# A language-model tower: the place of ScalarE's copies of the turned normed rows in slots 7 and 0 of a group

## The chip, the cores and the metric

The kernel runs on one core of one Trainium2 chip. The metric is the device time in microseconds (us), median of 3 runs. TensorE is called PE, VectorE DVE, ScalarE ACT, GpSimd POOL and SyncE SP.

## The reference

32 sequences of 128 tokens with 192 features go through an embedding with layer norm and four residual layers, each on the layer norm of the rows. Everything is fp32. The change lies in the stage that computes the first two and the first half of the third:

```python
h = tok_ref(x, mask, tok_w, pos_w, type_w, gamma, beta)              # embedding, layer norm
h = h + attn_ref(layernorm(h), Wq, Wk, Wv)                           # one head, causal
h = h + soft_experts(layernorm(h), phi, ln_g, ln_b, w1, b1, w2, b2)  # 64 experts x 16 slots
h = h + attn12(layernorm(h), w_qkv, w_proj, b_proj)                  # 12 heads, rotary
h = h + routed_experts(layernorm(h), router_w, w1, b1, w2, b2)       # 8 experts, top 1

# soft_experts, first half
phi_n  = phi * rsqrt(sum(phi**2, axis=0) + 1e-6)
logits = einsum('bmd,npd->bmnp', x, phi_n)       # 1024 slots (columns) per token
D      = softmax(logits, axis=1)                 # over the tokens
C      = softmax(logits, over all 1024 slots)    # used at the end of the layer
Xs     = einsum('bmd,bmnp->bnpd', x, D)          # the slots' inputs, then 64 experts, then C
```

## The kernel before, in words

The program has four stages one after the other: the tower (`tower_phase`, to about 338 us), the 64 soft experts, the combine and twelve-head attention stage, and the 8 routed experts. Only the tower is touched.

The 32 sequences are 8 groups of 4. The 1024 slots of the soft experts are 8 columns of 128. `each_slot` walks `t` from 0 to 11 and within each `t` eight places `s` from 0 to 7, which are called slots of the group here. At one `t` three groups are in work: `e = t` is embedded and normed, `a = t - 1` goes through the attention, `x = t - 2` gets the layer norm for the soft experts. Beside them one column runs per slot, in three steps: `n0` (its logits are made), `n1 = n0 - 1` (its weights are transposed), `n2 = n0 - 2` (the slots are summed). The first column begins at t = 2, s = 5. Every engine has its own program with the same walk and a function `slot`, and its instructions run in the order written there; engines meet only at semaphores.

What PE does in a slot, in this order: `logits_of(n0)` (five matmuls of 512 columns into bank 0 or 6, line 115 through the helper `matmuls`), `turn_weights(n1)` (four transposes into bank 1, L1050; waits for ACT's exponentials of the slot before), `slot_sums(n2)` (L1057; waits for ACT's copy of the transposed weights and for `stage_ready`, ACT's copy of the sums of the slot before), and after that what the attention needs: in slot 1 `queries`, in slot 2 `scores`, and so on. At the end of slot 6 it calls `turn_x(e, 0)`, and at the end of slot 7 `turn_x(e, 1)`: four transposes each (L955) of the normed rows `xn` (named e_rows in the trace) into bank 5, first the first 128 features, then the last 128 (64 and a repeat of them). Both use the same bank, so `turn_x(e, 1)` waits until ACT has copied the first half out (`pe.wait_ge(xT_took, 2 * e + 1)`). From t = 4 on, slot 0 ends with `turn_max` (L1027, `f = t - 4`), which also writes bank 5 and waits until ACT has copied the second half (`pe.wait_ge(xT_took, 2 * min(f + 4, NG))`).

What ACT does in a slot, in this order: `evict`, then for the column `take_turned(n1)` (copy of the transposed weights, L895), `exps(n0)` (four exponentials, L879; waits for DVE's column maximum `col_max`), `keep_logits(n0)` (L889), `take_sums(n2)` (L901, named slot_stage). In slot 7 `evict` holds the copy of the first half of the turned rows (L842, named e_x_full<-bank, semaphore `xT_took`); in slot 0 of the next `t` it holds the copy of the second half (L842) and then the rounding of both halves into `xThi` (L851, named e_x_hi, 1,024 columns, semaphore `xT_hi_ready`). In slots 2 to 6 it holds other copies.

What DVE does in slot 0, in this order: the column maximum (L760), the running maximum (L737), then `attn(a, 0)` (L681 and L682; waits for `xT_hi_ready`, makes `xT_split` for PE's `queries` in slot 1), then the statistics of group x and of group e (L619 to L624), which POOL turns into reciprocal roots. Slot 1 begins again with a column maximum (L760), on which ACT's exponentials of slot 1 wait. SP stores the kept logits and the slot sums as ACT makes them.

There are no columns in t = 0 and t = 1 at s = 7, and none in t = 1 and t = 2 at s = 0.

Of the kernel before, what the change touches and what calls it, by code (L numbers as in the profile page):

```python
# [97 lines left out]
def round_rest(act, stacked, rest):  # L98

    two = rest.rearrange("p (i n) -> p i n", i=2)  # L100
    act.activation(even(stacked[0:DR]), two[0:DR], ACT.Copy)
    return act.activation(odd(stacked[DR:P]), two[DR:P], ACT.Copy)
# [311 lines left out]
def tower_phase(nc, ins, T, small):  # L414
# [4 lines left out]
    with ExitStack() as ctx:  # L419
# [96 lines left out]
        with nc.Block() as block:  # L516
# [304 lines left out]
            def _(act):  # L821
# [18 lines left out]
                def take(ready, value, out, src, took):  # L840
                    act.wait_ge(ready, value)
                    act.activation(out, src, ACT.Copy).then_inc(took, 1)  # L842

                def evict(e_before, e, a, x, s):
                    if s == 7 and e is not None:
                        past(act, v_done, 2 * e)
                        take(xT_done, 2 * e + 1, xT[:, 0, :], b5, xT_took)
                    if s == 0 and e_before is not None:
                        take(xT_done, 2 * e_before + 2, xT[:, 1, :], b5, xT_took)
                        act.wait_ge(xT_took, 2 * e_before + 2)  # L850
                        act.activation(xThi[:], xT[:], ACT.Copy).then_inc(xT_hi_ready, 1)  # L851
                    if s == 2 and a is not None:
                        past(act, score_done, a)
                        take(q_done, 2 * a + 1, qT0[:], b7, q_took)
                    if s == 2 and a is not None:
                        take(q_done, 2 * a + 2, qT1[:], b4, q_took)
                    if s == 3 and x is not None:

                        past(act, logits, NC * (x - 1))
                        take(x3T_done, 2 * x + 1, T["x_hi"][x % 2][:], b5, x_hi_took)  # L860
                    if s == 4 and x is not None:
                        past(act, logits, NC * (x - 1))
                        act.wait_ge(x3T_done, 2 * x + 2)
                        round_rest(act, T["x_hi_over_lo"][x % 2], b5[:, 0:2 * P]).then_inc(x_hi_took, 1)
                    if s == 4 and a is not None:
                        past(act, av_done, 2 * a)
                        take(v_done, 2 * a + 1, v[:, 0:2, :], pair(b4), v_took)
                    if s == 5 and a is not None:
                        take(v_done, 2 * a + 2, v[:, 2:4, :], pair(b7), v_took)
                    if s == 6 and a is not None:  # L870
                        take(pT_done, a + 1, pT[:], b7, pT_took)

                def exps(n):
                    act.wait_ge(col_max, n + 1)

                    past(act, turned, n - 1)
                    for j in range(GB):
                        js = slice(j * P, (j + 1) * P)
                        last = act.activation(ls[:, n % 2, js], logits_bank(n)[:, js], ACT.Exp,  # L879
                                              bias=nmc[:, n % 2, j:j + 1])  # L880
                    last.then_inc(exped, 1)

                def keep_logits(n):
                    if n == 2:
                        act.wait_ge(T["xm_filled"], 16 * NE1 * CAP // (4 * P))
                    past(act, kept_stored[n // 2 % 3], 16 * (n // 6))

                    past(act, run_max_ready, run_maxes(n - 5) if n > 5 else 0)
                    act.activation(kept_columns(n), group4(logits_bank(n)), ACT.Copy).then_inc(kept_ready, 1)  # L889

                def take_turned(n):
                    act.wait_ge(turned, n + 1)

                    past(act, sums_done, n - 1)
                    act.activation(disp[:, n % 2, :], b1, ACT.Copy).then_inc(disp_ready, 1)  # L895

                def take_sums(n):
                    act.wait_ge(sums_done, n + 1)

                    past(act, stored[n % 3], 16 * (n // 3))  # L900
                    act.activation(stage[:, n % 3, :, :].rearrange("p (k j) d -> p k j d", k=2), U,  # L901
                                   ACT.Copy).then_inc(stage_ready, 1)

                def slot(t, s, e, a, x, n0, n1, n2, f):
                    evict(a, e, a, x, s)
                    if n1 is not None:
                        take_turned(n1)
                    if n0 is not None:
                        exps(n0)
                        keep_logits(n0)  # L910
                    if n2 is not None:
                        take_sums(n2)
                    if s == 3 and a is not None:
                        act.wait_ge(score_max, a + 1)
                        past(act, pT_done, a)
                        for j in range(GB):
                            last = act.activation(ex[:, j, :], sm[:, j, :], ACT.Exp, bias=nmx[:, j:j + 1],
                                                  accum_out=ssum[:, j:j + 1])
                        last.then_inc(exp_done, 1)
                    if t == LAST and s == 6:  # L920
                        small.first_take(act, 0, (b4, b7))
                        small.first_w1_hi(act)
                    if t == LAST and s == 7:
                        small.first_take(act, 1, (b4, b7))
                    if (s, e) in ((7, 1), (1, 2)):
                        k = e - 1
                        act.wait_ge(phi_scaled, k + 1)
                        act.activation(T[f"phi_hi{k}"][:], T[f"phiT{k}"][:], ACT.Copy).then_inc(phi_hi_ready, 1)

                each_slot(slot)  # L930
                act.wait_ge(nm_turned, 1)
                act.activation(nm_rows[:], b5[0:NB, 0:P], ACT.Copy).then_inc(nm_rows_ready, 1)
# [170 lines left out]
def past(eng, sem, value, wait=None):  # L1103

    if not isinstance(value, int) or value > 0:
        if wait:
            wait(eng, sem, value)
        else:
            eng.wait_ge(sem, value)
# [964 lines left out]
```

## Time and profile before

| | us |
|---|---|
| median of 3 runs | 1396.27 (1396.11 to 1398.48) |
| the profiled execution, device time | 1397.63 |
| its span in the trace | 1395.9 |
| busy in the span: PE / PEld / DVE / ACT / POOL | 1320.4 / 1175.0 / 974.7 / 951.6 / 253.5 |
| mean granted PE clock | 0.981 of full |

PEld is PE's weight load, which runs beside its matmuls. A row of the timeline gives the start of an instruction or of a run of equal ones, its length, engine, source line, output and inputs; in brackets stands how long the engine was idle before it and what released it. The end of a matmul is modelled, and matmuls overlap, so the distance of two starts says more than the lengths. A helper's line (L115, L842) stands for several callers; the tile's name tells them apart. Some tiles of the tower use buffers of the later stage and carry their names (e_x_full, e_x_hi, e_rows).

### The profile page before, as it was taken

The page shows a single profiled execution, that of the slowest core. Times are in us where ns is not written, and L with a number is a line of the kernel's source. Part 1 is how long each engine was busy: PE and PEld are TensorE (multiplying, and loading weights), DVE is VectorE, ACT ScalarE, POOL GpSimd, SP SyncE. Part 2 cuts the span into 40 slices and gives each one's busy share as a digit, 9 for nine tenths or more (in the row PEclk, how much of TensorE's full clock was granted, in tenths as well). Part 3 has the DMA queues.
Part 4 walks back from the last instruction along what each step waited for, and adds up shares of the span by engine and source line. Part 5 has one row for each costly group of instructions (what it writes and reads, how often), then busy time and mean ns, then how long its engine had stood idle before and what let it go on. Part 6 is the DMA issues. An engine that isn't in the chain of part 4 may idle for free. (4 is left out here: it accounts for less than half of the span.)

```text
span 1395.9 us, 29574 instructions
## 1 busy us (share of the span) xinstructions
PE 1320.4 (95%) x8926; PEld 1175.0 (84%) x8926; DVE 974.7 (70%) x2977; ACT 951.6 (68%) x2361; POOL 253.5 (18%) x284
## 2 busy tenths in 40 slices
PE   8799999998999999999999999799999999879995
PEld 6578888886898998998998998689889889768895
DVE  7888888555777777777777773688888888632331
ACT  1488888887676666666666663588888888735551
POOL 5321200000111111111111110012212212211344
PEclk9899999999999999999999999999999999989998
DMA  6144444455666666666666665545545547015641
GB/s 202 41 151 164 163 152 152 158 194 187 187 199 199 192 196 196 193 197 198 192 196 196 195 185 180 153 137 159 161 137 156 157 132 216 16 47 126 151 72 17
DMA packets 179715, 219.99 MB, mean 158 GB/s; under 512 B 23428, under 2 KB 146538, under 8 KB 179616
## 3 DMA queue, kind: packets, MB, share of 16 engines
q1 hardware_dynamic: 146224, 178.61, 41.6%
q10 hardware_dynamic: 25712, 33.19, 7.1%
q0 software_dynamic: 7680, 6.95, 2.5%
q8 instruction: 52, 0.85, 0.3%
q14 instruction: 47, 0.39, 0.1%
HBM read 141.31 MB, written 79.90 MB: 158 GB/s over the span
## 5 line engine op out<-in xcount | busy, mean ns | idle before, releaser
L1296 PE MATMUL bank<-e_w,e_h_full 128*128 128x192 f32 x1920 | 324.7, 326 | 0.4
L1296 PEld LDWEIGHTS bank<-e_w,e_h_full 128*128 128x128 f32 x1920 | 310.6, 190 | 1.7 <-ACT e_h_full L1370 1.3
L1370 ACT ACTIVATE e_h_full<-bank,e_b 128x512 f32<-128x512 f32 x240 | 165.2, 689 | 166.0 <-PE bank L115 166.0
L1234 POOL TENSOR_TENSOR e_ln_rstd<-e_ln_var_eps,minus_half 128x4 f32<-128x4 f32 x62 | 62.5, 1008 | 440.8 <-DVE e_ln_var_eps L1420 440.8
L1777 ACT ACTIVATE probs<-bank,head_neg_max 128x128 f32<-128x128 f32 x384 | 134.9, 392 | 7.8 <-DVE head_neg_max L1873 5.8
L1427 DVE TENSOR_SCALAR e_rows<-e_slot_sums,e_ln_mean_var,e_ln_rstd 128x192 f32<-128x192 f32 x248 | 77.5, 376 | 77.6 <-POOL e_ln_rstd L1234 77.6
L1339 ACT ACTIVATE e_x_full<-bank,e_ln_shift,e_ln_gain 128x512 f32<-128x512 f32 x124 | 76.5, 667 | 42.9 <-issue 37.6
L1057 PE MATMUL bank<-x,dispatch_weights 128*128 128x193 f32 x512 | 96.0, 329 | 7.2 <-ACT slot_stage L901 6.2
L115 PE MATMUL bank<-e_x_hi,e_w1hi 128*128 128x512 f32 x216 | 98.0, 454 | 2.7 <-ACT e_h_full L1370 1.7
L1657 PE MATMUL bank<-slot_outputs_then_w_part,combineT 128*128 128x193 f32 x512 | 92.5, 333 | 2.5 <-ACT combineT L1769 2.1
L1057 PEld LDWEIGHTS bank<-x,dispatch_weights 128*128 128x128 f32 x512 | 82.3, 190 | 11.2 <-issue 11.2
L1657 PEld LDWEIGHTS bank<-slot_outputs_then_w_part,combineT 128*128 128x128 f32 x512 | 83.1, 189 | 9.0 <-issue 9.0
L760 DVE TENSOR_REDUCE column_neg_max<-bank 128x4 f32<-128x512 f32 x64 | 44.2, 691 | 65.9 <-PE bank L115 65.4
L1777 ACT ACTIVATION_READ_ACCUMULATOR probs<-bank,head_neg_max 128x1 f32 x384 | 89.1, 232 | 0.0
L879 ACT ACTIVATE slot_exp<-bank,column_neg_max 128x128 f32<-128x128 f32 x256 | 72.9, 374 | 22.1 <-DVE column_neg_max L760 22.0
L1454 DVE TENSOR_TENSOR e_stage<-bank,e_b 128x768 f32<-128x768 f32 x64 | 61.3, 958 | 35.4 <-PE bank L1296 35.3
L115 PE MATMUL bank<-e_x_hi_over_lo,e_w1hi 128*128 128x512 f32 x216 | 86.0, 398 | 0.0
L115 PE MATMUL bank<-e_x_hi,e_w1lo 128*128 128x512 f32 x216 | 85.5, 396 | 0.0
L115 PE MATMUL bank<-e_x_lo,e_w1hi 128*128 128x512 f32 x216 | 85.4, 396 | 0.0
L115 PE MATMUL bank<-e_x_hi_over_lo,e_w1lo 128*128 128x512 f32 x216 | 85.1, 394 | 0.0
L1602 POOL TENSOR_TENSOR ln_rstd<-ln_var_eps,minus_half 128x1 f32<-128x1 f32 x64 | 35.9, 561 | 211.0 <-DVE ln_var_eps L1942 153.8
L122 PE MATMUL bank<-spare_operand 128*128 128x512 f32 x229 | 64.1, 428 | 8.4 <-PEq L1558 4.2
(286 smaller groups left out, 3127.7 us busy)
## 6 DMA issues: line engine op xcount, KB each, us to landing
slot_sums<-slot_stage SPq DMA_DIRECT2D x64, 386.0 KB, 3.2
e_slot_sums<-slot_sums SPq DMA_DIRECT2D x64, 386.0 KB, 3.6
slot_outputs<-e_stage ACTq DMA_DIRECT2D x64, 384.0 KB, 3.6
slot_outputs_then_w_part<-slot_outputs SPq DMA_DIRECT2D x32, 768.0 KB
e_w<-in_w SPq DMA_DIRECT2D x64, 288.0 KB, 2.9
slot_logits<-kept_logits SPq DMA_DIRECT2D x32, 512.0 KB
slot_logits<-slot_logits SPq DMA_DIRECT2D x32, 512.0 KB, 3.4
e_w1raw<-in_w SPq DMA_DIRECT2D x80, 192.0 KB, 2.7
```

Of the source, the lines that this page charges most:

```text
L115: last = pe.matmul(out, w, m, start=n == 0, stop=n == len(pairs) - 1, **kw)
L122: pe.matmul(out, T["spare"][:, 0:P], T["spare"][:], start=True, stop=True)
L879: last = act.activation(ls[:, n % 2, js], logits_bank(n)[:, js], ACT.Exp, bias=nmc[:, n % 2, j:j + 1])
L1057: last = pe.matmul(U[:, j // 2, j % 2, :], disp[:, n % 2, j * P:(j + 1) * P], x3[n // NC % 3][:, j, 0:1 + D], start=True, stop=True)
L1234: pool.tensor_tensor(rs[u][:], ve[u][:], half[:], ALU.pow).then_inc(rstd_ready, 1)
L1296: last = pe.matmul(ybank(u)[:, j // 2, (j % 2) * D:(j % 2 + 1) * D], hf[:, k, js], w2s[u][:, k, :], start=k == 0, stop=k == MT - 1)
L1339: last = act.activation(xf[:, k, 0:c], bank[:, k, 0:c], ACT.Identity, bias=lnb[:, k, ds(n, 1)], scale=lng[:, k, ds(n, 1)])
L1370: act.activation(hf[:, m, :], hbank(u, m), act_fn, bias=b1s[:, m, ds(n, 1)]).then_inc(acted, 1)
L1427: last = dve.tensor_scalar(rows[u][:, j, :], features_of(sums[u], j), mv[u][:, j, 0:1], rs[u][:, j:j + 1], ALU.subtract, ALU.mult)
L1454: dve.tensor_tensor(y_out[:, part], y_in[:, part], b2s[u][:].unsqueeze(1).unsqueeze(1) .broadcast_to([P, 2 // halves, 2, D]), ALU.add).the ...
L1657: last = pe.matmul(bank[:, 0, 0:D + 1], cT[:, c, :], ysb[u][:, c, :], start=c == 0, stop=c == NC - 1)
L1777: last = act.activation(pr[:, s, g, :], bank[:, 4 + s, g * P:(g + 1) * P], ACT.Exp, bias=nmx[:, s, g:g + 1], accum_out=esum[:, s, g:g + 1])
```

## The change

ACT's `slot` calls `evict` at the head of a slot. Now it does so in slots 1 to 6 only; in slots 7 and 0 it calls it behind the four column steps. No instruction, buffer, semaphore or wait value is added or removed, and the other engines' programs are the same.

```diff
                 def slot(t, s, e, a, x, n0, n1, n2, f):
-                    evict(a, e, a, x, s)
+                    if s not in (0, 7):
+                        evict(a, e, a, x, s)
                     if n1 is not None:
                         take_turned(n1)
                     if n0 is not None:
                         exps(n0)
                         keep_logits(n0)
                     if n2 is not None:
                         take_sums(n2)
+                    if s in (0, 7):
+                        evict(a, e, a, x, s)
                     if s == 3 and a is not None:
```

## Rows read from the trace of the kernel before

**Rows 1.** One stretch: length; busy (instructions) of PE, PEld, DVE, ACT, POOL; PEclk; DMA; GB/s.

```profile
150.00:200.00 50.00, 47.30 (x299) 42.52 (x297) 42.43 (x123) 40.85 (x104) 9.03 (x9) 1.00 0.44 160
```

**Rows 2.** Waits, 0 to 480 us: total us, times, longest us.

```profile
PE bank L1057 <- ACT slot_stage L901: 6.2, 10, 1.0
...
PE bank L955 <- ACT e_x_full L842: 0.7, 1, 0.7
```

**Rows 3.** Timeline of ACT, t = 5 slot 7 to t = 6 slot 1.

```profile
177.63 0.60 ACT L842 ACTIVATE e_x_full<-bank 128x512 f32<-128x512 f32 x1 [0.29 <-PE bank L955]
179.17 0.60 ACT L895 ACTIVATE dispatch_weights<-bank 128x512 f32<-128x512 f32 x1 [0.94 <-PE bank L1050]
...
181.14 0.85 ACT L901 ACTIVATE slot_stage<-bank 128x772 f32<-128x772 f32 x1
181.84 0.65 ACT L842 ACTIVATE e_x_full<-bank 128x512 f32<-128x512 f32 x1
182.51 1.06 ACT L851 ACTIVATE e_x_hi<-e_x_full 128x1024 fp32r<-128x1024 f32 x1
183.48 0.58 ACT L895 ACTIVATE dispatch_weights<-bank 128x512 f32<-128x512 f32 x1
...
185.43 0.85 ACT L901 ACTIVATE slot_stage<-bank 128x772 f32<-128x772 f32 x1
...
189.07 1.15 ACT L879 ACTIVATE slot_exp<-bank,column_neg_max 128x128 f32<-128x128 f32 x4 [2.30 <-DVE column_neg_max L760]
```

**Rows 4.** Timeline of PE, the same slots to slot 2.

```profile
178.97 1.48 PE L1057 MATMUL bank<-x,dispatch_weights 128*128 128x193 f32 x8
180.28 0.60 PE L955 MATMUL bank<-ident,e_rows 128*128 128x128 f32 x4
...
181.88 0.60 PE L1050 MATMUL bank<-ident,slot_exp 128*128 128x128 f32 x4
...
183.63 0.60 PE L1027 MATMUL bank<-ident,running_max 128*128 128x128 f32 x4
...
186.43 1.55 PE L1057 MATMUL bank<-x,dispatch_weights 128*128 128x193 f32 x8 [0.60 <-ACT slot_stage L901]
187.68 0.53 PE L115 MATMUL bank<-e_x_hi,M_hi 128*128 128x512 f32 x1
...
191.55 1.55 PE L1057 MATMUL bank<-x,dispatch_weights 128*128 128x193 f32 x8
```

**Rows 5.** Timeline of DVE, slots 0 and 1.

```profile
183.61 0.69 DVE L681 TENSOR_TENSOR e_x_lo<-e_x_full,e_x_hi 128x512 fp32r<-128x512 f32 x1 [0.24 <-ACT e_x_hi L851]
...
188.34 0.69 DVE L760 TENSOR_REDUCE column_neg_max<-bank 128x4 f32<-128x512 f32 x1
```

**Rows 6.** Timeline of ACT, t = 3 slot 0 (first) and t = 8 slot 1.

```profile
76.67 1.06 ACT L851 ACTIVATE e_x_hi<-e_x_full 128x1024 fp32r<-128x1024 f32 x1
...
258.26 0.84 ACT L901 ACTIVATE slot_stage<-bank 128x772 f32<-128x772 f32 x1
```

**Rows 7.** Timeline of DVE, t = 3 slot 0.

```profile
79.12 0.69 DVE L681 TENSOR_TENSOR e_x_lo<-e_x_full,e_x_hi 128x512 fp32r<-128x512 f32 x1
```

**Rows 8.** Timeline of PE, t = 8 slot 2.

```profile
260.70 1.48 PE L1057 MATMUL bank<-x,dispatch_weights 128*128 128x193 f32 x8
```

**Rows 9.** Timeline of PE, three of its pauses, elsewhere in the span.

```profile
48.68 0.79 PE L115 MATMUL bank<-e_x_hi,M_hi 128*128 128x512 f32 x1 [2.40 <-DVE e_x_hi_over_lo L682]
...
885.86 0.88 PE L1702 MATMUL bank<-ident,qk_padded 128*128 128x128 f32 x6 [2.19 <-DVE qk_padded L1949]
...
1208.62 0.62 PE L115 MATMUL bank<-onehot,upto 128*128 128x128 f32 x2 [2.14 <-ACT probs L1777]
```

**Rows 10.** Stretches behind these pauses, columns as in rows 1.

```profile
51.00:52.00 1.00, 1.00 (x4) 0.82 (x3) 1.00 (x2) 0.29 (x1) 0.69 (x2) 0.64 0.09 28
886.00:888.00 2.00, 2.00 (x13) 1.74 (x13) 0.68 (x2) 0.81 (x1) 0.81 (x4) 1.00 0.34 109
1210.00:1212.00 2.00, 2.00 (x11) 2.00 (x10) 0.55 (x2) 1.18 (x2) 0.44 (x2) 0.50 0.00 0
```

## The prediction, on record before the changed kernel was run

> **What bounds the kernel now.** I read the page's first part, then the waits of the first third, then the timelines of ACT, PE and DVE over one turn of the tower, from slot 7 of one t to slot 2 of the next. The first part has PE busy for 95% of the span, and a stretch in the tower shows the same, 47.30 of 50 us at a granted clock of 1.00 [rows 1]; an edit on ACT costs or gains only through what PE then waits for. In the waits of the tower the largest one of PE on ACT is for the copy of the slot sums, 6.2 us in ten waits. For the copy that the change moves, PE waited once, 0.7 us [rows 2]. So the copies sit well today, and the wait that the change could shorten is worth 6.2 us at the very most.
>
> The timelines show the order in time. In slot 7 ACT copies the first half at 177.63, right after PE has turned it, and then sits idle for 0.94 us until PE has transposed the column's weights; the column work starts at 179.17 [rows 3]. PE comes to the second half's transposes at 180.28, long after the copy's end at 178.23, and goes through without a pause [rows 4]. In slot 0 the second copy starts at 181.84, the rounding ends at 182.51 + 1.06 = 183.57, and DVE takes it at 183.61: DVE was waiting for it, 0.24 us [rows 3, 5]. From there a chain runs on DVE to the column maximum of slot 1 at 188.34, for which ACT's exponentials wait 2.30 us [rows 3, 5]. The copy of the sums behind them lets PE's slot sums of slot 2 start at 191.55 [rows 4]. So two things end on the moved instructions: PE directly, through bank 5, and that chain through DVE.
>
> **The change, slot 7.** Nothing is added or removed. The first copy now stands behind the four column steps. Those can't start sooner: what they wait for is PE's transposes at 179.17, and ACT was idle ahead of them [rows 3]. So the gain on ACT is nothing, the 0.60 us of the copy merely leave an idle place. The copy starts where the last column step lets it, at 181.84 (the copy behind the same step in slot 0 started then [rows 3]), and ends at 182.44. From ACT's end to PE's start I take 0.15 us: the copy of the sums ends at 185.43 + 0.85 = 186.28 and PE starts at 186.43 [rows 3, 4]. PE's second transposes therefore start at about 182.60 in place of 180.28, 2.32 us later. PE has nothing else to do: its slot sums are over at 178.97 + 1.48 = 180.45 [rows 4], the transposes are next in its order, and all of the next slot's logits are queued behind them. That is a pause of 2.15 us.
>
> **The change, slot 0.** PE's transposes of the column's weights ended at 181.88 + 0.60 = 182.48, 2.20 us after the second half's began [rows 4]. Now they end at 182.60 + 2.20 = 184.80, and ACT's column work starts at 184.84. It was at 183.48, because the second copy and the rounding stood ahead of it; the move gains 1.0 us here against the transposes' end, and loses it again at once. The column work takes 181.84 - 179.17 = 2.67 us from its first start to the next instruction's [rows 3], so the second copy starts at 187.51. From its start to the end of the rounding it takes 183.57 - 181.84 = 1.73 us [rows 3], so the rounding ends at 189.24, 5.67 us later than before.
>
> PE is done with slot 0's sums by 180.45 + 3.35 + 2.32 = 186.12 (3.35 us is the distance from 180.28 to 183.63, one slot of PE [rows 4]) and `turn_max`, next in its order, waits for the second copy: 187.51 + 0.64 + 0.15 = 188.30 in place of 183.63. That is a second pause, of 2.18 us. The 0.60 us pause ahead of slot 1's sums goes [rows 4], since the copy of the sums now ends earlier, at 187.6. PE's queries in slot 1 come at 188.30 + (187.68 - 183.63) - 0.76 = 191.59, where 0.76 is that pause seen from the start that it would otherwise have had. They need DVE's two instructions, over 1.4 us behind the rounding at 190.7, and don't wait. PE alone would be 3.91 us late.
>
> But the DVE chain decides. It starts 5.67 us later, and it had no pause to give back but the one at its head: the maximum of slot 1 moves from 188.34 to 194.01, ACT's exponentials from 189.07 to 194.74, and PE's sums of slot 2 from 191.55 to 197.22, with two short pauses ahead of them. From slot 2 on all three engines are late by the same 5.67 us, and PE is back to running without slack; there is nothing left to catch up with. POOL's roots, the gathers and SP's stores hang on these engines and move along; no DMA is issued from ACT here.
>
> **How often.** A slot 7 and the next slot 0 with column work occur in six pairs: t = 2/3 to t = 7/8. In t = 0 and 1 there are no columns and the order is as it was. Four pairs are as worked out, 22.7 us. In the first pair DVE took the rounding only at 79.12 though it was ready at 76.67 + 1.06 = 77.73 [rows 6, 7]: 1.35 us of cover beyond the hand-over, so 4.32 us. In the last pair there is no group to embed any more, DVE's chain is shorter, and PE's sums of slot 2 at 260.70 did not wait: the copy ahead of them ended at 258.26 + 0.84 = 259.10 [rows 6, 8]. That is 1.45 us of cover after the hand-over: 4.22 us. Sum: 31.2 us.
>
> **The clock.** The tower runs at the full granted clock [rows 1], and the change puts twelve pauses of 2.15 to 2.18 us in. Three pauses of that size stand in the trace [rows 9]: after 2.40 us at 48.68 and after 2.14 us at 1208.62 PE came back at the lower level, 1.2 GHz (0.64 in the mean of 51 to 52, 0.50 at 1210 to 1212), after 2.19 us at 885.86 at the full one, 2.4 GHz [rows 10]. Two of three came back low, so I take the clock to fall in four of the six pauses in slot 7. The low stretch after 48.68 lasted to about 51.7 (a mean of 0.64 is 0.72 us at half), so 3.0 us in which 1.5 us of work is lost. There it all lies on the path, since ACT's column work waits for PE's transposes: 4 x 1.5 = 6.0 us. Bounds: 0 and 9.0. After the pause in slot 0 PE has 5.67 - 3.91 = 1.76 us of slack against the DVE chain, which covers the 1.5 us: nothing.
>
> By the Trainium skill (TensorE: Matmul & The Clock Gate, Why this matters for your kernels) only pauses longer than these need be avoided to hold the full clock; by that the sum would stay at 31.2. Two of the three rows above speak against it, one for it, so it is a rival below.
>
> **The sum.** 31.2 + 6.0 = 37.2 us. On the profiled execution, 1397.63, that gives 1434.8; it was 1.36 us above the median of its runs, so on the median 1396.27 it is 1433.5. I say 1433.
>
> **Rivals.**
> - The clock holds in all twelve pauses: 1396.3 + 31.2 = 1427.5. For it: the pause at 885.86 [rows 9]. Against: the two others.
> - The clock falls in all six slot-7 pauses, and sometimes in slot 0 beyond the slack: 31.2 + 9.0 + about 2 = 42, 1438.5.
> - Only PE's own waits count and DVE's chain catches up: six times 3.91, 23.5 us, 1419.8. Against: DVE waited at the head of its 4.73 us from 183.61 to 188.34, and ACT at their end [rows 3, 5].
> - Other sign, faster: in slot 0 ACT's column work no longer stands behind 1.73 us of copies. The copy of the sums would end 1.0 us earlier and the 0.60 us pause ahead of slot 1's sums would go, with no loss elsewhere: 6 x 0.6 = 3.6 us, 1392.7. It decides on one point: whether the first copy is done when PE comes to the second transposes, at 180.28. It would have to be 2.2 us earlier than the order on ACT lets it.
> - The change does nothing, because PE's pauses fall on time that it had idle anyway: 1396.3. The trace shows no such idle time at 180.28 or 183.63 [rows 4].
>
> **How the numbers follow.** Forecast (2 to 5 falls of the clock) 0.53, clock holds 0.22, clock falls always 0.15, PE alone 0.06, no change 0.02, faster 0.02. The forecast's case spans 1429 to 1437; the range takes in the neighbours less the ends, 1424 to 1440. A change of 0.2%, 2.8 us, is about what can be told from none. Slower by more than that has 0.96, within it 0.02, faster 0.02.
>
> **What would show it.** In the trace after: six waits of PE at L955 and five at L1027 (from t = 4 on) on ACT's e_x_full, each 2.0 to 2.3 us; the copy of slot 7 right behind slot_stage; ACT idle ahead of the weights' copy in slot 0; DVE idle some 3.6 us ahead of L681 (0.24 + 5.67 - 2.32); the distance of two e_x_hi starts 5.7 us longer than before, more where the granted clock shows 0.5; the stages after the tower as long as before. It is wrong if the L955 waits are missing or well below 2 us, if the period grows by some 4 us only (then DVE's chain had slack), or if the clock costs over 2 us a pair.

## The result, and the profile after

The changed kernel takes 1437.22 us (median of 4 runs, 1432.4 to 1438.73) against 1397.38 for the kernel before beside it: ratio 1.0284, 95% interval 1.0263 to 1.0304, some 39.8 us slower. The forecast was 1433, in a range of 1424 to 1440. The profiled execution took 1438.32 us, its span is 1436.6, 40.7 more than before. ACT's first gelu of the experts starts at 383.2 in place of 343.6, so 39.6 us of that were lost in the tower; the stages behind it lost 1.1 us, which I don't explain. That is less than the executions of one kernel differ by (1396.1 to 1401.7 for before).

The profile page's first part, columns as in the table of before. PE's idle time grew by 28.0 us (103.5 against 75.5). The other 12.7 us are PE being busy for longer with as many instructions, at a mean granted clock of 0.975 in place of 0.981; ACT and DVE did the same work as before.

```profile
PE 1333.1 (93%) x8926; PEld 1183.0 (82%) x8926; DVE 974.0 (68%) x2977; ACT 950.1 (66%) x2361; POOL 252.5 (18%) x284
```

The waits of the changed kernel from 0 to 500 us, columns as in [rows 2]. Before, the first was 1.8 us in six waits, the second 0.7 us in one (the same one stands here as the seventh, beside six of 2.08 us), the third did not occur, and the fourth was 0.7 us in one. Line numbers behind the change are three higher than before, so L958 are the transposes of the normed rows, L1030 is `turn_max`, L1053 the transposes of the weights and L1060 the slot sums. The last line shows what the change saved: the old wait for slot_stage fell from 6.2 to 4.6 us.

```profile
DVE e_x_lo L681 <- ACT e_x_hi L851: 23.3, 7, 4.0
...
PE bank L958 <- ACT e_x_full L842: 13.2, 7, 2.1
...
PE bank L1030 <- ACT e_x_full L842: 10.1, 5, 2.2
...
PE bank L1053 <- ACT slot_exp L879: 5.6, 4, 2.0
...
PE bank L1060 <- ACT slot_stage L901: 4.6, 8, 1.0
```

One pair of slots in the timeline of the changed kernel, t = 3 slot 7 to t = 4 slot 1, first PE. It answers to [rows 4].

```profile
112.87 1.48 PE L1060 MATMUL bank<-x,dispatch_weights 128*128 128x193 f32 x8
116.42 0.66 PE L958 MATMUL bank<-ident,e_rows 128*128 128x128 f32 x4 [2.08 <-ACT e_x_full L842]
...
122.16 0.63 PE L1030 MATMUL bank<-ident,running_max 128*128 128x128 f32 x4 [2.17 <-ACT e_x_full L842]
...
131.07 1.55 PE L1060 MATMUL bank<-x,dispatch_weights 128*128 128x193 f32 x8 [0.32 <-ACT slot_stage L901]
```

The same pair on ACT, answering to [rows 3]. The copy of slot 7 stands right behind slot_stage and PE's transposes start 0.05 us after its end; then ACT idles 2.34 us, because PE's next weights come late. In slot 0 the same happens again.

```profile
115.03 0.85 ACT L901 ACTIVATE slot_stage<-bank 128x772 f32<-128x772 f32 x1
115.73 0.64 ACT L842 ACTIVATE e_x_full<-bank 128x512 f32<-128x512 f32 x1
118.71 0.60 ACT L895 ACTIVATE dispatch_weights<-bank 128x512 f32<-128x512 f32 x1 [2.34 <-PE bank L1053]
...
121.37 0.64 ACT L842 ACTIVATE e_x_full<-bank 128x512 f32<-128x512 f32 x1
122.05 1.06 ACT L851 ACTIVATE e_x_hi<-e_x_full 128x1024 fp32r<-128x1024 f32 x1
...
128.60 1.14 ACT L879 ACTIVATE slot_exp<-bank,column_neg_max 128x128 f32<-128x128 f32 x4 [2.38 <-DVE column_neg_max L760]
```

And on DVE, answering to [rows 5]. It idles 3.57 us for the rounded rows (0.24 before), and its 4.73 us to the next column maximum are as long as they were.

```profile
118.28 0.69 DVE L760 TENSOR_REDUCE column_neg_max<-bank 128x4 f32<-128x512 f32 x1 [2.84 <-PE bank L115]
...
123.14 0.69 DVE L681 TENSOR_TENSOR e_x_lo<-e_x_full,e_x_hi 128x512 fp32r<-128x512 f32 x1 [3.57 <-ACT e_x_hi L851]
...
127.87 0.69 DVE L760 TENSOR_REDUCE column_neg_max<-bank 128x4 f32<-128x512 f32 x1
```

The granted clock (the third number from the right) in eight stretches of the changed kernel, columns as in [rows 1]. Four of the six pauses in slot 7 were followed by the lower level (158, 202, 244, 288); those that ended at 76.07 and 116.42 were not. The stretch at 124 follows the pause ahead of turn_max. Two more, at 174 and 260, follow pauses in slot 2, one pair of which stands in the PE lines below the table.

```profile
116.00:118.00 2.00, 1.57 (x9) 1.39 (x10) 0.00 (x0) 0.37 (x1) 0.00 (x0) 1.00 0.50 198
124.00:126.00 2.00, 2.00 (x8) 1.70 (x8) 1.90 (x9) 0.38 (x1) 0.00 (x0) 0.50 0.16 57
158.00:160.00 2.00, 2.00 (x7) 1.51 (x6) 0.07 (x1) 0.00 (x0) 0.00 (x0) 0.50 0.05 19
174.00:176.00 2.00, 2.00 (x9) 1.91 (x9) 2.00 (x5) 1.14 (x4) 0.00 (x0) 0.52 0.50 198
202.00:204.00 2.00, 2.00 (x8) 1.62 (x7) 0.53 (x1) 0.00 (x0) 0.00 (x0) 0.50 0.02 8
244.00:246.00 2.00, 2.00 (x8) 1.51 (x8) 0.35 (x1) 0.00 (x0) 0.00 (x0) 0.56 0.00 0
260.00:262.00 2.00, 2.00 (x11) 1.91 (x10) 2.00 (x6) 1.24 (x5) 0.00 (x0) 0.50 0.19 67
288.00:290.00 2.00, 2.00 (x9) 1.80 (x8) 1.29 (x2) 0.57 (x2) 0.00 (x0) 0.50 0.00 0
```

```profile
172.12 0.66 PE L1053 MATMUL bank<-ident,slot_exp 128*128 128x128 f32 x4 [1.44 <-ACT slot_exp L879]
173.41 2.26 PE L1060 MATMUL bank<-x,dispatch_weights 128*128 128x193 f32 x8 [0.62 <-ACT slot_stage L901]
```

The distance of two roundings (e_x_hi, L851 here) is the tower's period and the best ruler for what follows. This table is made from the timelines of ACT; the first column is the kernel before, the others are what each kernel of the next section adds to it. I call a period clean when no stretch of low clock lies in it that delays it.

```
rounding t ->  before  changed  slot 7  slot 0  filled  stats  filled+stats  behind exps
3 -> 4          36.04    +4.32   +0.88   +3.15   +5.94  +1.23         +1.29        +0.02
4 -> 5          34.73    +7.25   +3.42   +5.00   +5.65  +6.69         +3.48        +0.79
5 -> 6          35.07    +8.56   +2.92   +3.35   +7.25  +4.07         +3.51        +0.78
6 -> 7          34.72    +7.18   +1.94   +3.33   +5.60  +3.44         +3.47        +0.77
7 -> 8          34.72    +8.49   +1.99   +5.02   +5.66  +6.29         +3.50        +0.82
```

### The profile page after: what moved, and what is told of

Same layout as the page of the kernel before. It is cut to its first block and busy times, and to the rows that moved or that the text cites. A ratio compares the mean times of both kernels' runs of the same rounds, so it can differ in the third digit from the quotient of the medians.

```text
span 1436.6 us, 29574 instructions
## 1 busy us (share of the span) xinstructions
PE 1333.1 (93%) x8926; PEld 1183.0 (82%) x8926; DVE 974.0 (68%) x2977; ACT 950.1 (66%) x2361; POOL 252.5 (18%) x284
## 5 line engine op out<-in xcount | busy, mean ns | idle before, releaser
L1060 PE MATMUL bank<-x,dispatch_weights 128*128 128x193 f32 x512 | 98.3, 335 | 5.3 <-ACT slot_stage L901 4.6
L1060 PEld LDWEIGHTS bank<-x,dispatch_weights 128*128 128x128 f32 x512 | 84.9, 195 | 8.5 <-issue 8.5
L895 ACT ACTIVATE dispatch_weights<-bank 128x512 f32<-128x512 f32 x64 | 38.6, 603 | 54.9 <-PE bank L1053 53.8
```

Of the source, the lines that this page charges most:

```text
L1060: last = pe.matmul(U[:, j // 2, j % 2, :], disp[:, n % 2, j * P:(j + 1) * P], x3[n // NC % 3][:, j, 0:1 + D], start=True, stop=True)
```

## The experiments

All times of before are those that ran beside the experiment on the same chip. "..." in a cut of code or of a profile stands for lines left out.

**Slot 7 alone.** ACT's copy of the first half behind the column steps, slot 0 as before. The cut is against the kernel before.

```diff
-                    evict(a, e, a, x, s)
+                    if s != 7:
+                        evict(a, e, a, x, s)
...
+                    if s == 7:
+                        evict(a, e, a, x, s)
```

> Only slot 7's copy stands behind the column steps, slot 0 is as before. Theory (PE waits in bank 5, then the chain copy, rounding, DVE, ACT decides): PE pauses 2.1 us at its second transposes of the normed rows, six times; the rounding in slot 0 comes only 1.4 us later (the copy waits for PE's transposes, 183.24 in place of 181.84), so 1.4 to 1.6 us in four pairs, 0.7 in the first, 1.6 in the last: 8 us, and 4 of 6 falls of the clock at 1.5 us: 14 us over before. Rival (each copy costs its own PE pause, 2.3 us a pair): 14 us without any fall of the clock, 20 with. So the period of the rounding where the clock holds tells them apart: +1.4 or +2.3.

Measured: 1409.33 against 1397.05, ratio 1.0090 (1.0071 to 1.0109), 12.3 us. In the two clean periods (6 to 7 and 7 to 8) the addition is 1.94 and 1.99 us: neither 1.4 nor 2.3. PE paused six times 2.08 us, and three of these pauses were followed by the lower clock, not four. So the total, 2 us under the 14 expected, hides a higher price per period behind one fall less. The timelines of this kernel, PE, ACT and DVE, show the term that I had missed; the last line is the same column maximum in the kernel before:

```profile
189.35 0.66 PE L958 MATMUL bank<-ident,e_rows 128*128 128x128 f32 x4 [2.08 <-ACT e_x_full L842]
```

```profile
190.68 1.06 ACT L851 ACTIVATE e_x_hi<-e_x_full 128x1024 fp32r<-128x1024 f32 x1
```

```profile
191.21 0.69 DVE L760 TENSOR_REDUCE column_neg_max<-bank 128x4 f32<-128x512 f32 x1 [2.84 <-PE bank L115]
191.82 0.68 DVE L737 TENSOR_TENSOR running_max<-running_max,kept_logits 128x512 f32<-128x512 f32 x1
192.42 0.69 DVE L681 TENSOR_TENSOR e_x_lo<-e_x_full,e_x_hi 128x512 fp32r<-128x512 f32 x1
```

```profile
182.08 0.69 DVE L760 TENSOR_REDUCE column_neg_max<-bank 128x4 f32<-128x512 f32 x1 [0.54 <-PE bank L115]
```

The rounding is done at 191.74, but DVE comes to it only at 192.42, without idling: its column maximum waits for PE's logits, which come 2.3 us late behind the pause. From that maximum to L681 it is 1.21 us where it was 1.53 (183.61 - 182.08, with DVE's wait of 0.24 in it, [rows 5]), so 2.3 - 0.3 = 2.0 us. The chain decides, as in the theory, but it can begin in two places: at ACT's rounding, or at DVE's column maximum of slot 0, which waits for PE. Slot 7's pause enters at the second.

**Slot 0 alone.** ACT's copy of the second half and the rounding behind the column steps, slot 7 as before. The cut is against the kernel before.

```diff
-                    evict(a, e, a, x, s)
+                    if s != 0:
+                        evict(a, e, a, x, s)
...
+                    if s == 0:
+                        evict(a, e, a, x, s)
```

> Only slot 0's copy and rounding stand behind the column steps. Theory: ACT's column work starts 1.0 us earlier, the rounding ends 3.35 us later, PE pauses 2.2 us at turn_max, and the DVE chain makes it 3.35 us a pair, 2.0 and 1.9 in the first and last: 17 us; a fall of the clock at turn_max is covered by 1.8 us of slack and costs nothing: 17 to 19 us over before, more than slot 7 alone though PE's pause is as long. Rival (PE's pause alone counts): 2.3 - 0.8 = 1.6 us a pair, 8 to 10 us, plus the clock.

Measured: 1420.32 against 1397.05, 1.0162 (1.0142 to 1.0182), 23.3 us, above what I expected. The rival is out: it wanted 1.6 us a pair. The periods confirm 3.35 us (3.35, 3.33), and confirm that a low clock behind turn_max is free: the period 5 to 6 holds one from 160.4 to 163.8 and adds 3.35. The excess has two parts. Three of slot 2's pauses were followed by the lower clock; in the periods 4 to 5 and 7 to 8 that cost 1.6 to 1.7 us each, behind double pauses (two close together, first PE lines below). The third, in the period 3 to 4, began at 88.7, right behind a single pause of 1.98 us (last PE line). And in the first pair DVE took the rounding 3.46 us later after all (81.92 against 79.12, with the whole trace 0.66 earlier), not 2.0. The cover of 1.35 us was there, but the rounding itself came 4.83 us later in place of 3.35: DVE's column maximum, behind its sum for the group being embedded (L633), held ACT's column steps for 1.37 us, and the rounding now stands behind those.

```profile
127.77 0.66 PE L1053 MATMUL bank<-ident,slot_exp 128*128 128x128 f32 x4 [1.08 <-ACT slot_exp L879]
129.05 2.29 PE L1060 MATMUL bank<-x,dispatch_weights 128*128 128x193 f32 x8 [0.63 <-ACT slot_stage L901]
```

```profile
88.58 1.00 PE L1053 MATMUL bank<-ident,slot_exp 128*128 128x128 f32 x4 [1.98 <-ACT slot_exp L879]
```

```profile
81.92 0.69 DVE L681 TENSOR_TENSOR e_x_lo<-e_x_full,e_x_hi 128x512 fp32r<-128x512 f32 x1 [3.38 <-ACT e_x_hi L851]
```

**The long pauses filled.** The changed kernel and, ahead of the late transposes, nine matmuls whose result is never used, in each of the eleven long pauses.

```diff
+                    if n2 is not None and (s == 7 and e is not None or s == 0 and None not in (a, f)):
+                        pe.wait_ge(kept_ready, n0)
+                        keep_busy(pe, T, logits_bank(n0 + 1), 9)
```

> The changed kernel, with nine matmuls of 512 columns on the spare operand in each of the eleven long pauses (ahead of the second transposes in slot 7, ahead of turn_max in slot 0), into the logits bank that is free then. Theory: the order on ACT is as in the changed kernel, so its 31 us stay, but the clock stays at the full level behind these pauses: 31 to 34 us over before, 1428 to 1431, each period of the rounding without a fall 5.67 us longer than before. Rival (the clock costs nothing, the rest is DVE or ACT work that got slower): as the changed kernel, 1437, or more by the matmuls.

Measured: 1430.58 against 1397.05, 1.0243 (1.0219 to 1.0266), 33.5 us, where the changed kernel lost 39.8. The rival, a clock that costs nothing, is out. In the same view as above no stretch behind a filled pause is below 1.00. Three clean periods add 5.65, 5.60 and 5.66 us, against 5.67 worked out. The periods 3 to 4 and 5 to 6 hold a low stretch by slot 2's pauses, which were not filled (at 91 and 173). Two stretches of this kernel, one behind a filled pause and one of the two low ones:

```profile
122.00:126.00 4.00, 3.89 (x23) 3.08 (x22) 1.59 (x4) 2.65 (x5) 0.00 (x0) 1.00 0.65 232
172.00:176.00 4.00, 3.37 (x14) 3.08 (x13) 4.00 (x13) 3.14 (x8) 0.00 (x0) 0.62 0.25 99
```

**DVE's statistics ahead.** The changed kernel, DVE fills its 3.6 us of idle time in slot 0.

```diff
+                    first = s == 0 and x is not None and n0 is not None
+                    if first:
+                        slot_input(x, s)
+                        if e is not None:
+                            embed(e, s)
                     if a is not None:
                         attn(a, s)
-                    if x is not None:
+                    if x is not None and not first:
                         slot_input(x, s)
...
-                    elif e is not None:
+                    elif e is not None and not first:
                         embed(e, s)
```

> The changed kernel, with DVE's statistics of slot 0 (of groups x and e) ahead of its two instructions on the rounded rows, in the 3.6 us that it waits for them. Theory: the DVE chain is 3.5 us shorter behind the rounding, then PE's own 3.9 us a pair bind in place of 5.67: 22 us without the clock, and the pause ahead of slot 2's transposes is gone; the clock costs 6 us behind slot 7 and now also up to 5 behind slot 0, since the slack there is gone: 1424 to 1431, below the changed kernel. Rival (only PE's waits on bank 5 count, the DVE chain does not): no change against the changed kernel, 1437.

Measured: 1421.77 against 1397.05, 1.0174 (1.0143 to 1.0204), 24.7 us: 15 us below the changed kernel, from an order on DVE alone. The rival that the chain doesn't count is out. DVE's next column maximum now starts 1.27 us behind the rounded rows, where it was 4.73 (first lines below). The slack that covered a fall of the clock behind turn_max is gone with it, as expected: the two periods that hold such a fall beside one behind slot 7 add 6.69 and 6.29 us, the one with a fall behind slot 7 alone 4.07. The total is 2 us better than the low end I gave; the one clean period adds 3.44, not 3.91. Of these 0.47 us 0.3 are a pause in slot 2 of the kernel before that no bracket shows: the sums at 191.55 [rows 4] stood 0.74 us behind the transposes at 190.81 (last line below), where 0.44 is the usual distance, and it is gone in the kernel with both repairs (203.33 to 203.77). The rest is not explained.

```profile
202.34 0.69 DVE L681 TENSOR_TENSOR e_x_lo<-e_x_full,e_x_hi 128x512 fp32r<-128x512 f32 x1 [0.70 <-ACT e_x_hi L856]
...
203.61 0.68 DVE L760 TENSOR_REDUCE column_neg_max<-bank 128x4 f32<-128x512 f32 x1
```

```profile
190.81 0.60 PE L1050 MATMUL bank<-ident,slot_exp 128*128 128x128 f32 x4
```

**Both repairs.** The two diffs above together.

> The changed kernel with both the spare matmuls in the long pauses and DVE's statistics ahead. Theory: only PE's own waits are left, 3.9 us in five pairs and 2.6 in the first, with the clock at the full level all along: 22 us over before, 1419. Rival (the two repairs act on the same loss): the better of the two alone.

Measured: 1415.51 against 1397.65, 1.0124 (1.0105 to 1.0143), 17.9 us, 4 under the 22 expected. The two repairs add up (6.3 and 15.1 us alone, 21.9 together): they act on two losses. With the clock at 1.00 from 68 to 360 us the four periods behind the first add 3.47 to 3.51. I take this to be PE's own share, the two waits on bank 5, and it is 0.4 us a pair below what I had worked out. The rest of the 4 us seems to lie between executions: the profiled one was one of the two slower of five (1418.79, against 1414.92 to 1415.51 for the other three), and by its trace the tower is 19.8 us longer than before (first gelu at 363.4).

```profile
68.00:360.00 292.00, 279.89 (x1672) 246.12 (x1670) 198.40 (x534) 229.98 (x574) 36.43 (x36) 1.00 0.43 153
```

**Slot 7's copy behind the exponentials.** The kernel before, with the copy two steps down.

```diff
-                    evict(a, e, a, x, s)
+                    if s != 7:
+                        evict(a, e, a, x, s)
                     if n1 is not None:
                         take_turned(n1)
                     if n0 is not None:
                         exps(n0)
+                    if s == 7:
+                        evict(a, e, a, x, s)
+                    if n0 is not None:
                         keep_logits(n0)
```

> Slot 7's copy two steps down only, behind the four exponentials, slot 0 as before. Theory: PE pauses about 1.2 us at its second transposes, but in slot 0 ACT is only 0.5 us late (the copy's time now lies on the busy part), and PE's 1.2 us goes into the pause ahead of slot 1's sums: 0.5 us a pair, 2 to 3 us over before, no fall of the clock. Rival (PE's pause at bank 5 is the loss): 1.2 us a pair, 7 us.

Measured: 1400.77 against 1397.65, 1.0018 (1.0007 to 1.0030), 3.1 us, just above the 2 to 3 that I expected; 0.77 to 0.82 a period behind the first. PE pauses 0.9 us in each slot 7, and no low clock follows in any of the six. The size comes again from the second place where the chain begins: the maximum comes 1.1 us late (it stands 1.85 us behind PE's transposes, and these 4.41 us behind those of slot 6, where it was 1.80 and 3.34), 0.3 is absorbed (1.21 us to L681 in place of 1.53), 0.8 is left. The rival's 7 us are out, but less is absorbed than I thought.

**Half of the rounding in slot 7.** The other direction, on the kernel before.

```diff
                         take(xT_done, 2 * e + 1, xT[:, 0, :], b5, xT_took)
+                        act.wait_ge(xT_took, 2 * e + 1)
+                        act.activation(xThi[:, 0, :], xT[:, 0, :], ACT.Copy)
...
-                        act.activation(xThi[:], xT[:], ACT.Copy).then_inc(xT_hi_ready, 1)
+                        act.activation(xThi[:, 1, :], xT[:, 1, :], ACT.Copy).then_inc(xT_hi_ready, 1)
```

> The kernel before, with the rounding of the first half of the rows moved from slot 0 into slot 7 right behind its copy, where ACT is idle 0.94 us; slot 0 rounds 512 columns in place of 1,024. Theory (the chain rounding, DVE, column maximum, exponentials sets slots 1 and 2): it starts 0.46 us earlier and the pauses of PE ahead of slot 1's and slot 2's sums shrink: 0.4 us a pair, 2 to 2.5 us faster than before, 0.15%. Rival (PE alone bounds and the pauses have another cause): no change.

Measured: 1395.33 against 1397.65, 0.9977 (0.9966 to 0.9988): 2.3 us faster, as expected. The timeline of ACT shows where the work went, into the idle place of slot 7, and the second rounding, now 0.63 us long where the whole one took 1.06:

```profile
175.85 0.60 ACT L842 ACTIVATE e_x_full<-bank 128x512 f32<-128x512 f32 x1 [0.29 <-PE bank L957]
176.48 0.63 ACT L849 ACTIVATE e_x_hi<-e_x_full 128x512 fp32r<-128x512 f32 x1
177.39 0.60 ACT L897 ACTIVATE dispatch_weights<-bank 128x512 f32<-128x512 f32 x1 [0.27 <-PE bank L1052]
...
180.73 0.63 ACT L853 ACTIVATE e_x_hi<-e_x_full 128x512 fp32r<-128x512 f32 x1
```

**DVE's x_lo in slot 7 too.** On top of the last one; the first rounding signals a semaphore of its own, and DVE waits for that at the end of slot 7.

```diff
+                    if e is not None and s == 7:
+                        dve.wait_ge(first_hi, e + 1)
+                        past(dve, v_done, 2 * e)
+                        dve.tensor_tensor(xTlo[:], xT[:, 0, :], xThi[:, 0, :].bitcast(F32), ALU.subtract)
...
-                        dve.tensor_tensor(xTlo[:], xT[:, 0, :], xThi[:, 0, :].bitcast(F32), ALU.subtract)
```

> As the kernel with the first half rounded in slot 7, and DVE's first instruction on these rows (x_lo, 0.69 us) moved from slot 0 to the end of slot 7 too, where DVE was idle 0.54 us. Theory: what is left of PE's pauses ahead of the sums of slots 1 and 2 is 0.2 us each, so at most 0.4 us a pair more, and the DVE chain shrinks by 0.6: 1 to 2 us below the 1395.3 of that kernel, 0.3% below the kernel before. Rival: DVE's column maximum of slot 0 now comes 0.1 us late behind it and nothing is gained: 1395.3.

Measured: 1392.15, against 1399.59 for before in this job, 0.9954 (0.9940 to 0.9969). Against the 1395.33 of the last kernel it is 3.2 us in medians, but of another job and chip; by the ratios the step is 0.2%. By the traces the first gelu comes 1.5 us earlier than in the last kernel (339.4 against 340.9), within the 1 to 2 us expected. The rival, no gain at all, is unlikely by that, and by the pauses: ahead of the sums of slots 1 and 2 one of 0.17 us is left from t = 4 on, where the last kernel had five. The roundings of t = 4 and 5 are 33.96 us apart, of 5 and 6 34.07, of 6 and 7 33.94, 0.8 to 1.0 us below before. This is the best kernel of the study, faster than both.

## Why the prediction was right

**PE's wait on bank 5 in slot 7 and slot 0.** Worked out 2.15 and 2.18 us, measured 2.08 six times, and 2.17, 2.17, 1.86, 2.17, 1.74 in slot 0. The two short ones, 1.86 and 1.74, came in pairs where the clock had fallen behind slot 7's pause; two others in such pairs were 2.17 all the same, so that alone doesn't explain them. The hand-over from ACT is 0.05 us at the transposes of slot 7 (116.37 to 116.42), not 0.15; at turn_max it is 0.15 (122.01 to 122.16). The prediction speaks of twelve pauses; there are eleven, as its last paragraph has it, since turn_max begins at t = 4.

**The chain through DVE decides, 5.67 us a pair.** Shown: 5.60 to 5.66 in the clean periods of the filled kernel; and with DVE's order changed 3.5 us, so the chain's excess over PE's own waits is 2.2 us a pair. The prediction saw one place where this chain begins, ACT's rounding. In the changed kernel that is the one that decides; the experiments on slot 7 show the other.

**PE's own 3.91 us** was over-sized: 3.5 in the kernel with both repairs. I had subtracted the visible pause ahead of slot 1's sums but not the 0.3 us in slot 2; 0.1 stays open. It did not enter the sum.

**First and last pair.** In the changed kernel the first period adds 4.32, which is 5.67 less the first pair's cover of 1.35, and behind the last rounding 1.2 us came back (I had 1.45). Both covers hold. In slot 0 alone the first was there too, but the rounding came 1.5 us later than I had worked out, for a reason I had not seen, and that used it up.

**The clock, 6.0 us.** This is the term that was mis-sized, 6.0 against 8.8. That four of six pauses in slot 7 would be followed by the lower level came out, at 1.51 and 1.58 us where only one cost anything in a period (7.18 and 7.25 less 5.67). The price is shown; the number four is in part luck. It was taken from three rows, slot 7 alone had three of six and the statistics ahead four of six, and the changed kernel's own four executions lie between 1432.4 us at a mean clock of 0.980 and 1438.73 at 0.976. The reading that the tower runs at the full clock [rows 1] is true from 69 to 338 us only, which is where the pairs lie. That a fall behind turn_max is free came out too: 122.16 in the changed kernel, 160 in slot 0 alone. What I left unpriced are the "two short pauses" ahead of slot 2's transposes and sums: 1.44 or 1.05 us and 0.62 us, close together. Twice in the changed kernel the lower clock followed them, 1.3 us each (8.56 and 8.49 less 5.67 less 1.55). So the clock cost 1.58 + 2.89 + 1.51 + 2.82 = 8.8 us. With 31.2 that is 40.0, against 39.6 in the tower by its first gelu, or 40.2 counted from a common start, as the changed kernel's trace runs 0.6 us ahead when the columns begin. So the sum of the tower agrees to 0.5 us, for this one execution. One of the prediction's signs of being wrong, a clock that costs over 2 us a pair, came true in two periods (2.89 and 2.82), though not in the mean of the six pairs (1.5): there the clock was low twice in one period, which the sum had at nothing.

**The skill's rule** (the Trainium skill, TensorE: Matmul & The Clock Gate, Why this matters for your kernels), that only longer pauses than these need be avoided, does not hold here: of 18 pauses of 2.08 us in slot 7 of three kernels (changed, slot 7 alone, statistics ahead) 11 were followed by the lower level, and filling the pauses gave back 6.3 us (39.8 less 33.5). The measurement decides.

**The sign rival** would have needed the first copy done at 180.28; nothing of it was seen but the 1.6 us less of waits for slot_stage.

## What to carry to other kernels

Before an eviction is moved down an in-order engine, ask who waits for the bank that it frees and what that engine has queued behind this wait; here the copy stood in an idle place for nothing, and 0.6 us of it moved down cost 2 us a group through two engines. Follow the delay to the point where the engines meet again: the price was set by the longest way round (copy, rounding, DVE, maximum, exponentials), and a new order on one engine of that way, DVE, gave back 15 us of the 40. An idle place ahead of a wait is where work of the late chain belongs: the two kernels that moved work up into slot 7 were the only ones that gained, 2.3 us and 0.5% (against before in their own jobs).

## What I had not expected of the hardware

Short pauses can be followed by the lower clock too. In slot 2 of three kernels (changed, slot 0 alone, filled) there were eight double pauses of 1.04 to 1.09 us and then 0.62 or 0.63 us; three were followed by it, while none of the six single pauses of 0.9 us in slot 7 of the kernel with the copy behind the exponentials was. Where the first pause was longer, 1.4 to 2.0 us, it was four of five, but once the clock was low right behind the first pause, and once it fell during the second. So these counts are small, and that two pauses close together count like a long one is a reading, not shown: no run fills or removes the second pause alone. Nor is it every long pause: of eleven of 2.17 to 2.18 us ahead of turn_max (changed, slot 0 alone, statistics ahead) five were followed by it. Whether a given pause of 2.08 us is followed by it differs from one pair to the next in the same execution, with the same work around it; what decides that the runs don't show.
